# Cross-attentions of layers 2 to 4: the last context row subtracted from the others by GpSimd, the last key a constant, the last value added by feature

## What is computed

```python
# x: (64, 32, 256), context: (64, 257, 256), 16 heads of 16 features
q = (x @ Wq.T + bq).reshape(B, N, H, D)
k = (context @ Wk.T + bk).reshape(B, M, H, D)
v = (context @ Wv.T + bv).reshape(B, M, H, D)
scores = jnp.einsum('bnhd,bmhd->bhnm', q, k) * SCALE
bias = jnp.where(ctx_key_padding_mask[:, None, None, :] != 0, 0.0, neg)
attn = jax.nn.softmax(scores + bias, axis=-1)
out = jnp.einsum('bhnm,bmhd->bnhd', attn, v).reshape(B, N, C)
x = x + (out @ Wo.T + bo)          # x on the right is layer-normed first
```

## Time and profile before

| | |
|---|---|
| time, median of 3 runs | 3406.27 us (3396.41 to 3411.48) |
| span of the profiled execution | 3403.5 us |
| the same execution's own device time | not given beside the span |
| mean granted TensorE clock | 0.967 |
| TensorE busy | 3201.0 us, 94% |
| VectorE, ScalarE, GpSimd busy | 66%, 43%, 31% |
| layer 2's cross-attention | from 509 to 942 us |
| layer 3's | from 1727 to 2156 us |
| layer 4's | from 2645 to 3075 us |

### The profile page before, as it was taken

The page is one execution under the profiler, slowest core; times in us unless marked ns, Lnnn a source line. Parts: engine busy times, 40 slices in busy tenths (PEclk is TensorE's granted clock), DMA queues, the critical chain, the costliest instruction groups (busy, mean ns, idle before and its releaser), DMA issues. The chain is left out here.

```text
span 3403.5 us, 105614 instructions
## 1 busy us (share of the span) xinstructions
PE 3201.0 (94%) x39150; PEld 2569.5 (75%) x39150; DVE 2263.3 (66%) x7473; ACT 1458.3 (43%) x4212; POOL 1048.3 (31%) x1684
## 2 busy tenths in 40 slices
PE   8979899999996999999999999889999999998899
PEld 6758787788774888888878888776666778877676
DVE  4767326777757988888747777774334577777755
ACT  2325335666632333333336666552111455555432
POOL 0114112333343544444523333343110111114441
PEclk9989899999998999999999999988999999998799
DMA  6643332122103000000011111006111111110333
GB/s 226 219 169 156 115 112 63 56 71 59 64 32 128 3 2 2 2 2 2 2 31 42 52 45 56 2 27 231 47 46 67 36 40 41 43 42 2 99 104 113
DMA packets 145872, 225.26 MB, mean 66 GB/s; under 512 B 14216, under 2 KB 121480, under 8 KB 143816
## 3 DMA queue, kind: packets, MB, share of 16 engines
q1 hardware_dynamic: 138816, 203.16, 18.8%
q0 software_dynamic: 6816, 18.69, 1.5%
HBM read 201.03 MB, written 38.74 MB: 70 GB/s over the span
## 5 line engine op out<-in xcount | busy, mean ns | idle before, releaser
L3385 POOL TENSOR_TENSOR l1fu_second_weighed<-l1fu_second,l1fu_parts 128x256 bf16<-128x256 bf16 x384 | 273.1, 738 | 342.9 <-DVE l1fu_second L3628 336.0
L3437 PEld LDWEIGHTS l1fu_ps_u<-l1f_xnT_all,l1f_key_in 128*128 128x128 f32 x2048 | 249.4, 193 | 17.8 <-issue 11.6
L3437 PE MATMUL l1fu_ps_u<-l1f_xnT_all,l1f_key_in 128*128 (+1 forms) x2048 | 252.1, 277 | 9.1 <-issue 7.5
L3448 PE MATMUL l1fu_ps_y<-l1f_key_out,l1fu_units 128*128 128x256 f32 x1024 | 250.6, 389 | 1.6 <-DVE l1fu_units L3636 1.6
L3448 PEld LDWEIGHTS l1fu_ps_y<-l1f_key_out,l1fu_units 128*128 128x128 f32 x1024 | 185.7, 190 | 33.2 <-issue 6.2
L3501 ACT COPY l1fu_plane<-l1fu_ps_p 128x512 f32<-128x512 f32 x128 | 74.9, 585 | 252.9 <-PE l1fu_ps_p L3427 252.9
L3623 DVE TENSOR_TENSOR l1fu_first<-l1fu_index,l1fu_counted 128x1024 bf16<-128x1024 bf16 x128 | 165.4, 1292 | 20.1 <-PE l1fu_ps_p L3427 18.0
L3509 ACT ACTIVATE l1fu_units<-l1fu_ps_u 128x512 f32<-128x512 f32 x128 | 76.4, 597 | 147.9 <-PE l1fu_ps_y L3448 138.7
L1069 ACT ACTIVATE l1x_scores<-l1x_scores,l1x_minus_big 128x257 f32<-128x257 f32 x256 | 129.1, 516 | 12.0 <-DVE l1x_minus_big L1155 10.4
L1069 ACT ACTIVATE l2x_scores<-l2x_scores,l2x_minus_big 128x257 f32<-128x257 f32 x256 | 129.1, 516 | 12.1 <-DVE l2x_minus_big L1155 10.4
L1069 ACT ACTIVATE l3x_scores<-l3x_scores,l3x_minus_big 128x257 f32<-128x257 f32 x256 | 128.6, 505 | 10.9 <-DVE l3x_minus_big L1155 9.7
(11 more groups left out here) (755 smaller groups left out, 8514.7 us busy)
## 6 DMA issues: line engine op xcount, KB each, us to landing
rows_by_expert<-in_zeros_dram SPq DMA_DIRECT2D x1, 17544.0 KB
l0x_ctxT<-in_ctx_T_dram SPq DMA_DIRECT2D x32, 514.0 KB, 5.3
l0x_ctx_rows<-in_ctx_dram SPq DMA_DIRECT2D x64, 256.0 KB, 3.5
l0f_w<-in_L_ffn_w_dram SPq DMA_DIRECT2D x16, 1024.0 KB, 5.1
l1x_ctx_sb<-in_ctx_T_dram SPq DMA_DIRECT2D x60, 256.0 KB, 3.3
l2x_ctx_sb<-in_ctx_T_dram SPq DMA_DIRECT2D x60, 256.0 KB, 3.4
l3x_ctx_sb<-in_ctx_T_dram SPq DMA_DIRECT2D x60, 256.0 KB, 2.8
l1x_mask_raw<-in_mask_int_dram SPq DMA_DIRECT2D x16, 514.0 KB, 4.2
```

Of the source, the lines that this page charges most:

```text
L3385: last = nc.gpsimd.tensor_tensor(second_weighed[:, k % 2, part], second[:, k % 2], parts[:, 1 - par, part, TC * k:TC * k + TC].unsqueeze(2 ...
L3437: last = nc.tensor.matmul(ps_u[:, k % 2, j, :], key_in[:, c, JS * k + j, :], xnT_all[:, c, bass.ts(tile, P)], start=(c == 0), stop=(c == C ...
L3448: last = nc.tensor.matmul(ps_y, units[:, k, j, :], key_out[:, JS * k + j, :], start=(k + j == 0), stop=(k == K - 1 and j == JS - 1))
```

## The change

It does five things in the three stages.

- GpSimd subtracts each batch's last context row from its 256 other rows, in place in SBUF, before they are projected (`less_last_key`, one operation of 128 partitions x 512 elements for each batch). For the first tile this is done at the end of the sublayer before (`shift_first_context`, behind all else that GpSimd does there), for the others in turn t of the tile before (`shift_context`). `keys` on TensorE waits for this subtraction, no longer for the load.
- The last key, column `K2` of `kT`, is the key projection's bias (or zero) for all batches. It is filled once a stage; `k_tail`, `put_tail_keys` and the key half of `next_tail_projections` are gone.
- `tail_share` is gone: GpSimd's operation, its transpose on TensorE, its half of ScalarE's copy.
- `weigh` on VectorE multiplies the product's result by the shares first and adds the last value as a scalar by feature together with the two halves: three operations instead of four.
- The values' bias now comes with the last value alone, so `keep_values` is a plain copy.

Three smaller effects follow from the code. `turn_shares` waits for `o_weighed`, the first operation of `weigh`, where it waited for `o_with_last`; `put_tail_values` waits for `oT_kept`; `maxima` no longer waits for `tail_share_ready`.

```diff
+    def less_last_key(self, rows, pack, tile, b):
...
+        return nc.gpsimd.tensor_tensor(rows, rows, pack["ctx_tail"][:, :, at].broadcast_to([P, C, KEYS - 1]),
+                                       ALU.subtract)
+
+    def shift_first_context(self, pool):
...
+        pool.wait_ge(self.pack_loaded[number], 16)
+        for b in range(BT):
+            pool.wait_ge(self.context_loaded[number][b], 16)
+            self.less_last_key(self.first_context(number)[:, b], self.pack_of(number), 0, b).then_inc(
+                self.context_shifted[number][b], 1)
...
         pe.wait_ge(self.pack_loaded[number], 16)
-        for oc in range(C):
-            for c in range(C):
-                nc.tensor.matmul(keys[:, oc * B:oc * B + B], pack["k"][:, c, oc * P:oc * P + P], pack["ctx_tail"][:, c, :],
-                                 start=(c == 0), stop=(c == C - 1))
...
+            def shift_context(i, b):
+
+                pool.wait_ge(per_batch["ctx_loaded"][b], i * 16)
+                core.less_last_key(ctx_sb[:, b], pack, i, b).then_inc(per_batch["ctx_shifted"][b], 1)
...
-                pool.wait_ge(per_batch["exp_ready"][b], n)
-                nc.gpsimd.tensor_tensor(tail_share[:, b % 2], scores[:, b, :, K2].unsqueeze(2).broadcast_to([P, R, 32]),
-                                        core.table("same_half").unsqueeze(1).broadcast_to([P, R, 32]),
-                                        ALU.mult).then_inc(per_batch["tail_share_ready"][b], 1)
...
                     if not first and t == 0:
                         put_tail_values(i, n)
+                    if not last:
+                        shift_context(i + 1, t)
                     if ahead:
                         shares(ahead, before)
...
                     if not last and t == 1:
-                        put_tail_keys(i + 1, n + 1)
                         mask_bias(n + 1)
...
-                    pe.wait_ge(per_batch["ctx_loaded"][b], (n - 1) * 16)
+                    pe.wait_ge(per_batch["ctx_shifted"][b], n - 1)
...
-                    pe.wait_ge(per_batch["o_with_last"][before[0]], before[1])
-                pe.wait_ge(per_batch["tail_share_ready"][b], n)
-                nc.tensor.transpose(ps_share[:, P:2 * P], tail_share[:, b % 2].rearrange("p r d -> p (r d)"), ident)
+                    pe.wait_ge(per_batch["o_weighed"][before[0]], before[1])
...
-                for c in range(C):
-                    of_chunk = slice(64 * c, 64 * c + 64)
-                    last = nc.vector.scalar_tensor_tensor(lastT[:, of_chunk], shareT[:, b % 2, 1, of_chunk],
-                                                          v_last[:, c, b:b + 1], ps_out[:, of_chunk], ALU.mult,
-                                                          ALU.add)
-                last.then_inc(per_batch["o_with_last"][b], 1)
-                dve.wait_ge(per_batch["o_with_last"][b], n)
-                nc.vector.tensor_tensor(weighed[:].rearrange("p c h q -> p (c h q)"), lastT[:], shareT[:, b % 2, 0],
+                nc.vector.tensor_tensor(weighed[:].rearrange("p c h q -> p (c h q)"), ps_out, shareT[:, b % 2],
                                         ALU.mult).then_inc(per_batch["o_weighed"][b], 1)
...
-                nc.vector.tensor_tensor(oT[:, :, b, :], weighed[:, :, 0, :], weighed[:, :, 1, :], ALU.add).then_inc(
-                    per_batch["oT_kept"][b], 1)
+                for c in range(C):
+                    last = nc.vector.scalar_tensor_tensor(oT[:, c, b, :], weighed[:, c, 0, :], v_last[:, c, b:b + 1],
+                                                          weighed[:, c, 1, :], ALU.add, ALU.add)
+                last.then_inc(per_batch["oT_kept"][b], 1)
```

More of the change, by code:

```diff
@@ L110, in __init__ @@
         self.context_loaded = {n: [nc.alloc_semaphore(f"context_loaded{n}_{b}") for b in range(BT)] for n in (3, 6, 9)}
+        self.context_shifted = {n: [nc.alloc_semaphore(f"context_shifted{n}_{b}") for b in range(BT)] for n in (3, 6, 9)}
         self.tail_ready = {n: nc.alloc_semaphore(f"tail_ready{n}") for n in (3, 6, 9)}
@@ L129, in load_first_context, with tail_view @@
                     self.context_loaded[number][b], 16)
-    def tail_views(self, bank):
-        return bank[:, 256:256 + C * B], bank[:, 256 + C * B:256 + 2 * C * B]
+    def less_last_key(self, rows, pack, tile, b):
+        nc = self.nc
+        at = slice(b, b + 1) if isinstance(tile, int) and tile == 0 else bass.ds(tile * BT + b, 1)
+        return nc.gpsimd.tensor_tensor(rows, rows, pack["ctx_tail"][:, :, at].broadcast_to([P, C, KEYS - 1]),
+                                       ALU.subtract)
+    def shift_first_context(self, pool):
+        number = self.number + 1
+        if number not in self.context_loaded:
+            return
+        pool.wait_ge(self.pack_loaded[number], 16)
[3 more added lines that the diff above has]
+                self.context_shifted[number][b], 1)
+    def tail_view(self, bank):
+        return bank[:, 256:256 + C * B]
     def next_tail_projections(self, pe, bank):
@@ L140, in next_tail_projections @@
         nc, pack = self.nc, self.pack_of(number)
-        keys, values = self.tail_views(bank)
+        values = self.tail_view(bank)
         pe.wait_ge(self.pack_loaded[number], 16)
-        for oc in range(C):
-            for c in range(C):
-                nc.tensor.matmul(keys[:, oc * B:oc * B + B], pack["k"][:, c, oc * P:oc * P + P], pack["ctx_tail"][:, c, :],
-                                 start=(c == 0), stop=(c == C - 1))
         for oc in range(C):
@@ L724, in cross_attention @@
         big = sb("big", [P, BT, R])
-        share, tail_share = sb("share", [P, 2, R, 32]), sb("tail_share", [P, 2, R, 32])
-        shareT, lastT = sb("shareT", [P, 2, 2, P]), sb("lastT", [P, P])
+        share, shareT = sb("share", [P, 2, R, 32]), sb("shareT", [P, 2, P])
         probsT = sb("probsT", [P, 2, 2, R, P])
@@ L1144, in maxima @@
                 after(dve, per_batch["probs_turned_2"][b], n - 1)
-                after(dve, per_batch["tail_share_ready"][b], n - 1)
                 wait(dve, per_batch["scores_ready"][b], n)
@@ L1162, in keep_values @@
                 after(dve, per_batch["o_ready"][b], n - 1)
-                if "bv" in rows:
-                    last = nc.vector.tensor_tensor(v[:, b], src[:], rows["bv"][:].unsqueeze(1).broadcast_to(
-                        [P, 2, D]), ALU.add)
-                else:
-                    last = nc.vector.tensor_copy(v[:, b], src[:])
-                last.then_inc(per_batch["v_kept"][b], 1)
+                nc.vector.tensor_copy(v[:, b], src[:]).then_inc(per_batch["v_kept"][b], 1)
             def keep_probs(at, before2, draining):
@@ L3394, in _ @@
             all_turns(pool, turn)
+            core.shift_first_context(pool)
         @block.tensor
```

51 lines of the change are left out of this document (22 added, 29 removed).

## The result

| | before | after |
|---|---|---|
| time, median of 9 runs, us | 3399.37 (3392.49 to 3411.48) | 3376.81 (3368.30 to 3390.43) |
| profiled execution: its time, us | not given beside the span | 3378.24 |
| its span, us | 3403.5 | 3376.5 |
| its mean granted TensorE clock | 0.967 | 0.971 |

The ratio is 0.9937, with a 95% interval of 0.9919 to 0.9954, which is a gain of 16 to 28 us. The gain between the medians is 22.6 us; 21.3 were predicted, both 0.63%. The forecast of 3385 was counted from the first three runs, 3406.27.

A forecast was written before the change was run, and what follows sets the result against it. TensorE, with products back to back, was taken to bound the steady part; 19.8 + 1.7 + 0.8 - 1.0 = 21.3 us off 3406.3 gave 3385 us, 0.63% less, range 3377 to 3398.

The forecast's parts named there:

- The transposes: TensorE in the three stages: dropping tail_share's transpose saves 0.11 us in each of 60 turns a stage, 19.8 us.
- The last keys' projections: TensorE at the end of sublayers 2, 5 and 8: 0.83 us saved, two of three counted, 1.7 us.
- weigh in the last batch: VectorE at each stage's end, where all waits for it: 0.27 us less, three times, 0.8 us gained.
- The subtraction's price: GpSimd, 512 columns for each batch: taken as 1.04 to 1.1 us, from rows of shorter operations.
- The first tile's four: Subtractions at the end of sublayers 2, 5 and 8, 4 to 6 us, where GpSimd is idle: no cost.
- The stall behind the mask: Batch 2's keys in the two masked stages: 0.03 us a tile, 15 tiles each, -1 us; 0.08 us left.
- a consumer on another engine starts about 0.10 after GpSimd's end: Step for batch 2 behind the mask: subtraction ends at 1896.99, so its keys' weight load can start at 1897.09.
- Rival A: Batch 2's subtraction behind the mask is dearer: 3392 at 1.4 us, 3428 at 2.6; chance 0.08 near 1.9 to 2.6.
- sublayer 5's 1.408 us: Median of an in-place GpSimd addition of 256 columns, same operand form; would make the subtraction 2.6 us, the kernel 3428.
- Rival B: GpSimd holds VectorE up: 3388 to 3395 at a 1.4 us subtraction; chance 0.20 together with a moderately dearer subtraction.
- if VectorE gets in only behind them: Batch 0's additions wait for share, x_plus_bo and batch 1's subtraction; free at 1913.6, outputs still hold by 0.4 us.
- C: Transposes give nothing, as a chain over ScalarE or VectorE takes over: 3403; chance 0.12 with what is near no change.

The follow-up runs named there:

- e4: Changed kernel with one more GpSimd operation of 128 columns (0.40 us) ahead of batch 2's subtraction in each tile; 3384.84 us, ratio 0.9951.
- e5: Changed kernel with one more subtraction of 512 columns, to a spare buffer, ahead of batch 2's own in each tile; 3410.73 us, ratio 1.0035.
- e9: Changed kernel with one more subtraction of 512 columns ahead of batch 1's and of batch 3's own; 3380.06 us, a single run.
- e3: Changed kernel without the subtraction from tile 2 on, the keys waiting for the load again; 3377.58 us, ratio 0.9927.
- e6: Changed kernel with batch 2's subtraction ahead of the mask's bias instead of behind it; 3403.24 us, ratio 0.9996.
- e7: Changed kernel with batch 2's subtraction directly behind batch 1's, ahead of the share of turn 1; 3377.09 us, ratio 0.9939.
- e11: Changed kernel with batch 2's subtraction directly behind batch 1's, the same kernel as e7 run again; 3378.67 us, ratio 0.9922.

## Why the prediction was right, step by step

**The transposes: right, 19.8 predicted, 19.5 by the tile.** The step that carried the forecast was to count 0.11 us from start to start and not the 0.27 of the row. The 39 steady intervals show 16.9 us; for the 15 tiles a stage that the forecast counted, 0.434 x 15 x 3 = 19.5. With 0.27 it would have been 49.

**The last keys' projections: 1.7 predicted, 2.1 measured.** TensorE at the end of sublayer 5, to be held against the earlier trace rows:

```profile
1715.67 0.55 PE L164 MATMUL pair_bank<-weights 128*128 128x64 f32 x4
...
1718.75 2.68 PE L905 MATMUL l2x_ps_s<-weights,weights 128*128 128x256 f32 x8 [1.22 <-PEq L3769]
```

From the start of the last projections to the stage's first keys are 3.08 us now. Before, the first keys were these:

```profile
1727.71 1.97 PE L889 MATMUL l2x_ps_s<-weights,weights 128*128 128x256 f32 x8 [1.21 <-PEq L3773]
```

From 1723.75 that was 3.96: 0.88 less now. Sublayer 8's end gives 0.90 (2.53 for 3.43) and sublayer 2's 0.34 (3.62 for 3.96). I had counted two of three at 0.83; the third gave a part. This is read in one trace of each kernel; no experiment took the projections alone.

**weigh in the last batch: 0.8 predicted, 0.75 measured.** VectorE, to be held against the earlier trace rows:

```profile
2137.34 0.29 DVE L1188 TENSOR_TENSOR l2x_weighed<-pair_bank,l2x_shareT 128x128 f32<-128x128 f32 x1 [0.96 <-PE pair_bank L978]
2137.73 0.41 DVE L1196 SCALAR_TENSOR_TENSOR l2x_oT<-l2x_weighed,l2x_v_last 128x32 f32<-128x32 f32 x2
```

From 2137.34 to 2137.73 + 0.41 is 0.80 us, where it was 1.05 and 0.78 was forecast. The other two stages' last batches show the same rows, and three times 0.25 is 0.75. The three terms make 22.4 us; the medians are 22.6 apart. With an interval of 16 to 28 us, that these sums meet within 1.3 us and less is in part luck: the runs confirm the transposes, and the two small terms rest on the rows alone.

**The subtraction's price: right.** By line, all 180 of the tiles behind a stage's first:

```profile
L136 POOL TENSOR_TENSOR l1x_ctx_sb<-l1x_ctx_sb,weights x60: 1035/1043/1049, 535.1 to 911.0; 128x512 f32<-128x512 f32 x60
L136 POOL TENSOR_TENSOR l2x_ctx_sb<-l2x_ctx_sb,weights x60: 1040/1042/1050, 1740.2 to 2116.0; 128x512 f32<-128x512 f32 x60
L136 POOL TENSOR_TENSOR l3x_ctx_sb<-l3x_ctx_sb,weights x60: 1041/1042/1047, 2648.1 to 3023.7; 128x512 f32<-128x512 f32 x60
```

The forecast's line through two shorter operations (1.66 ns a column above 0.19 us) gave 1.04. The first tile's four were hidden, as said (in layer 2's stage they ran from 497.9 to 501.9, and its first keys start at 513.63). The Trainium skill's figure ("GPSIMD Engine Reference", section 3.1) was scaled down to an estimate of 1.3 us. A quarter of 4.497 is 1.12, and the forecast doesn't say what it added; the measurement decides for 1.04 in this form, with one operand spread along the columns. At 1.3 the stall would by e4's margin have been some 0.1 us a tile, 3 us.

**The stall behind the mask: the one term that was wrong, -1 us predicted, 0 measured.** By the forecast's own working 0.08 us were left between the subtraction and the weight load, which is no stall at all; the 0.03 us a tile that it counted even so came from no row. The margin was larger than 0.08, too: e4 and e5 gave 0.14 to 0.15. Most of the difference is the step "a consumer on another engine starts about 0.10 after GpSimd's end": that was read between GpSimd and VectorE, and towards TensorE it is 0.05 (e5). The other steps were good to 0.05 us: the mask was to start 0.2 us earlier behind the share, and it starts 0.15 earlier (1881.39 - 1880.91 = 0.48 for 0.63).

**Rival A** had the right place and nearly the right price at which the gain is gone: 1.86 us for the subtraction, or 0.74 above an edge at 1.12. By the margin of 0.14 the edge is at 1.18. In e5 work of 1.04 + 1.01 = 2.05 us cost 0.87 a tile and made the kernel 0.35% slower. What did not hold was the row that spoke for it, sublayer 5's 1.408 us: in these stages no subtraction took more than 1.05.

**Rival B** was half right. VectorE is held up, and by more than I had looked for. But the step "if VectorE gets in only behind them", behind the share, x_plus_bo and the subtraction back to back, does not hold (e9), and so the room was not 0.4 us. The copy of the probabilities, and the outputs that need it:

```profile
1876.27 0.69 DVE L1173 COPY l2x_probsT<-l2x_ps_p 128x512 f32<-128x512 f32 x1 [0.23 <-PE l2x_ps_p L957]
...
1878.62 0.65 PE L978 MATMUL pair_bank<-l2x_probsT,l2x_v 128*32 128x64 f32 x32
```

It ends at 1876.27 + 0.69 = 1876.96, 1.66 us ahead of the outputs.

The rule on the shared port pair, that the other engine is fully blocked for the whole instruction (the Trainium skill, "SBUF — State Buffer", "Who interferes with whom"), agrees beside the subtraction and x_plus_bo, one instruction at a time, and does not beside the mask's bias. I had weighed it for additions between two SBUF tensors alone. The same section of the Trainium skill also names operations that can take the second port with one SBUF tensor, `tensor_scalar` among them, and the norm is one: 1.08 us for 0.40. I had not looked for that. It cost nothing here, since even a norm 0.7 us later is not late.

**The chances.** The forecast was given 0.60, and its own range of 3379 to 3389 held the gain as measured (3406.3 - 22.6 = 3383.7), though not the median itself, 3376.81. What I could have known better is C: with all rows of TensorE back to back and the transpose inside the only short loop over another engine, 0.12 was much for it.

What stays open: why the mask's bias, 3.7 us long and reading SBUF, lets VectorE's addition through after 0.97, while the subtraction holds the norm to its end. Another pair of VectorE operations, `q_by_half`, was slowed beside the mask but not held to its end: it took 1.07 to 1.08 us beside it in e3 and in the kernel after, and 0.76 where GpSimd was idle. The mask's input is of one byte for each element in this stage; no run here varied that.

## What to carry to other kernels

On an engine whose instructions stand back to back, value an instruction by the distance to its successor's start, not by its duration: 0.11 against 0.27 us decided this forecast. Work moved to an idle engine is priced by its place: look for the longest operation that it will stand behind (here the mask's 3.7 us), compute the margin to the consumer, and if it is under a few tenths of a microsecond, put the work a few operations earlier, where it costs the same and risks less. And check both neighbours of such a long operation before moving anything across it: it had a deadline too, here 0.4 to 0.5 us away.

## What the runs showed of the hardware

- A VectorE `tensor_scalar` of 128x256 float32 with one SBUF tensor and two scalars by partition took 0.404 us alone and 1.08 beside a GpSimd subtraction of 1.04 us.
- VectorE got in between two GpSimd operations that followed each other directly: the additions that met x_plus_bo took 0.91 us with two subtractions queued behind it (e9) and 0.90 with one.
- GpSimd's end reached a waiting TensorE weight load in 0.05 us (e4 and e5, 60 of 60 tiles). VectorE started 0.10 us behind GpSimd's end in the earlier trace rows, and 0.17 behind the mask's bias in e6.
- In the first tile of layer 2's stage, behind a wait of 2.33 us, eight key products took 3.45 to 3.75 us in stretches with a granted clock of 0.50 to 0.57. The values' eight took 3.18 us where the clock was 0.65 and 1.89 in the execution where it came back to 1.00. In the steady part, at 1.00, both take 1.89.
- Two profiled executions of one kernel (e7, e11) were 17.5 us apart, and their 39 steady intervals agreed to 0.1 us in all: the whole difference lay outside the steady part.
